# GIN's later layers in a message-passing kernel: y in two float16 parts, and two source tiles side by side in TensorE's column halves

## The reference, cut to what matters

```python
for l in range(4):
    S = segment_sum(X[src], dst)                       # over 3125 nodes
    Z = (1 + eps[l]) * X + S
    h = relu(bn(Z @ W1[l].T + b1[l], g1[l], bt1[l]))   # 128 -> 32 channels
    h = relu(bn(h @ W2[l].T + b2[l], g2[l], bt2[l]))   # 32 -> 32
    X = h @ W3[l].T + b3[l]                            # 32 -> 128
```

## Time and profile before

| what | us |
|---|---|
| median of 3 runs | 2328.12 (2324.81 to 2331.11) |
| the profiled execution, its own time | 2327.49 |
| its span, first to last instruction | 2325.7 |
| mean granted TensorE clock | 0.791 |
| busy: TensorE matmul / weight load | 1891.2 / 1354.5 |
| busy: DVE / ACT / POOL | 1375.0 / 1154.5 / 1360.8 |
| GIN, from its first products to its last read-out | 259.6 to 566.0 |

### The profile page before, as it was taken

One profiled execution on the slowest core, in us unless ns is written; L12 is line 12 of the kernel. 1 busy time (PEld: TensorE's weight loads), 2 busy tenths in 40 slices (PEclk: granted clock), 3 DMA queues, 4 the chain that ended last, 5 costly groups with the idle time before them and its releaser, 6 DMA issues. The chain is left out here.

```text
span 2325.7 us, 42471 instructions
## 1 busy us (share of the span) xinstructions
PE 1891.2 (81%) x8329; PEld 1354.5 (58%) x8329; DVE 1375.0 (59%) x4159; ACT 1154.5 (50%) x2623; POOL 1360.8 (59%) x1337
## 2 busy tenths in 40 slices
PE   3888667787798989998879989989986666667666
PEld 2666435554788878888655545545565455555554
DVE  6999681113543444344256666576567777777775
ACT  2999111112266666666436055064044666566663
POOL 1000137774477777777417758858826777777771
PEclk9999698788755555555579999999987777777777
DMA  0000101111344444444311111111132222222221
GB/s 11 0 0 0 44 4 17 18 18 12 105 120 119 117 119 118 117 119 119 103 33 18 17 16 18 17 16 18 20 133 72 65 64 64 64 65 65 64 64 38
DMA packets 195681, 128.56 MB, mean 55 GB/s; under 512 B 138365, under 2 KB 177854, under 8 KB 194587
## 3 DMA queue, kind: packets, MB, share of 16 engines
q0 software_dynamic: 40256, 60.21, 12.0%
q1 hardware_dynamic: 151388, 58.11, 9.9%
q10 hardware_dynamic: 3841, 8.16, 1.0%
HBM read 106.83 MB, written 13.34 MB: 52 GB/s over the span
## 5 line engine op out<-in xcount | busy, mean ns | idle before, releaser
L2157 POOL DMA_INDIRECT adj<-h_rows,adj x416 | 396.5, 953 | 153.4 <-issue 75.3
L1208 POOL DMA_INDIRECT work<-p_rows,small x416 | 395.3, 950 | 126.8 <-issue 99.7
L1584 POOL DMA_INDIRECT edge_rows<-pay,small x289 | 352.3, 1219 | 89.3 <-issue 85.4
L2374 PE MATMUL ps<-adj 128*128 128x125 f32 x928 | 209.1, 363 | 163.5 <-DVE adj L2252 161.2
L1392 PE MATMUL ps<-work 128*128 x1024 | 299.5, 446 | 43.5 <-ACT work L1328 39.6
L2374 PEld LDWEIGHTS ps<-adj 128*128 128x128 f32 x928 | 173.2, 256 | 255.5 <-issue 152.4
L1392 PEld LDWEIGHTS ps<-work 128*128 128x128 f32 x1024 | 232.9, 316 | 66.5 <-issue 60.7
L1285 DVE TENSOR_TENSOR work<-ps,work 128x256 f32<-128x256 f32 x256 | 108.6, 424 | 252.3 <-PE ps L1392 123.1
L1403 PE MATMUL ps<-small,work 128*128 128x64 f32 x1024 | 244.9, 393 | 11.2 <-DVE small L1274 7.7
L1403 PEld LDWEIGHTS ps<-small,work 128*128 128x128 f32 x1024 | 240.8, 323 | 20.4 <-DVE small L1274 15.3
L1946 PE MATMUL ps<-adj,work 125*128 (+2 forms) x1008 | 204.8, 359 | 20.5 <-DVE work L1675 20.5
(11 more groups left out here) (395 smaller groups left out, 3163.7 us busy)
## 6 DMA issues: line engine op xcount, KB each, us to landing
work<-dst_all SPq DMA_DIRECT2D x256, 64.0 KB
work<-edge_attr SPq DMA_DIRECT2D x256, 64.0 KB
edge_rows<-pay,small POOLq DMA_INDIRECT x425, 2.7
work<-p_rows,small POOLq DMA_INDIRECT x416
adj<-h_rows,adj POOLq DMA_INDIRECT x416
adj<-adj SPq DMA_DIRECT2D x232, 24.0 KB
pay<-edge_pay SPq DMA_DIRECT2D x106, 46.9 KB
adj<-edge_rows ACTq DMA_DIRECT2D x1, 2496.0 KB
```

The lines of the kernel that those rows point to most:

```text
L1208: eng.indirect_dma_start(gathered[:, at:at + D], None, p_rows[:, :], bass.IndirectOffsetOnAxis(ap=src_i[:, c:c + 1], axis=0)).then_inc(s_g ...
L1584: eng.indirect_dma_start(edge_rows[:, :], bass.IndirectOffsetOnAxis(ap=place[:, k:k + 1], axis=0), pay[:, k * ROW:(k + 1) * ROW], None).th ...
L2157: eng.indirect_dma_start(gathered[:, at:at + D], None, h_rows[:, :], bass.IndirectOffsetOnAxis(ap=row3_i[:, c, DST_C:DST_C + 1], axis=0)). ...
L2374: ins = eng.matmul(SUM[v % 2], msg[b][:, k * D:(k + 1) * D], hot[b][:, k * P:(k + 1) * P], start=k == 0, stop=k == PAIR - 1)
```

## The change

- In layers 1 to 3 y is kept in two parts of float16, 2 x 32 columns (`parts16`): ACT reads out the high part, DVE subtracts once. The columns of `joined` are multiplied by a power of two (`power`), which DVE makes from a bound on |y| (`size`), and `merge` for these layers holds the inverse (`size` / `TOP`). The bound is made by six matmuls into `BOUND` from `limits` (of gamma and beta), `sizes` (of `JOIN`) and `abs_b` (of `ROWS`).
- The adjacency product of layers 1 to 3 is written out: for each two slots, and each piece, one matmul with 64 columns of weights writes PSUM partitions 0 to 63 and the next, of the other slot, partitions 64 to 127. Slot 24 stands alone. The copies to `S` and the products with `merge` take 128 rows.
- b3 W1 no longer goes in by the degree: after a layer's last statistics TensorE writes the scaled bias row into the banks of y (two matmuls with one row of weights, 512 and 288 columns), and y is added to it.
- The degree row is saved in GIN, by SP, after layer 0's copies and ahead of the places. Layer 1's copies wait for it; the layernorm's transfer and wait go.
- `GIN_TURNS` is 14, so `EACH` is 13.

```diff
-GIN_TURNS = 17
+GIN_TURNS = 14
...
+    limits, tmp3, abs_b = s_(GH, GL - 1), s_(GH, GL - 1), s_(1, (GL - 1) * GH)
+    size, power = s_(D, (GL - 1) * GH), s_(D, (GL - 1) * GH)
+    bias_row = s_(1, (GL - 1) * GH)
...
+    parts16 = Words(T[3])(P, NT * 2 * GH, F16).rearrange("p (s c) -> p s c", c=2 * GH)
...
+    h, fold, sizes = y_(D, LONG), y_(D, D), y_(GH, (GL - 1) * GH)
...
-    merge = [t_(3 * GH + 1, WIDE) for _ in range(GL)]
+    merge = [t_(D, WIDE) for _ in range(GL)]
+    one_row = Words(G["extra"], 1536)(1, D)
...
-    JOIN, ROWS, OWN = (ps[:, 7, 0:(GL - 1) * GH], ps[0:3 * GH + 1, 7, 128:128 + (GL - 1) * GH],
+    JOIN, ROWS, OWN = (ps[:, 7, 0:(GL - 1) * GH], ps[0:1, 7, 128:128 + (GL - 1) * GH],
                        ps[:, 7, 256:256 + GL - 1])
+    BOUND = ps[:, 7, 384:384 + (GL - 1) * GH]
...
+            eng.wait_ge(s_sa, len(ACT_P))
+            eng.wait_ge(s_sv, len(DVE_P))
+            eng.dma_start(G["deg_row"][:, :], S[3 * GH:3 * GH + 1, :]).then_inc(s_deg, 16)
             eng.wait_ge(s_places, 1)
             eng.dma_start(places[:, :], place_i).then_inc(s_saved, 16)
             eng.wait_ge(s_saved, 16)
+            eng.wait_ge(s_deg, 16)
             for b in SETS:
                 fill(0, b)
             with eng.Fori(1, GIN_TURNS) as q:
...
-            for r in b3_row:
-                ins = eng.memset(r, 0.0)
-            step(ins)
+            step(eng.memset(one_row, 1.0))
...
-            for m in merge:
+            for m in merge[0:1]:
                 for i in range(3):
                     eng.tensor_copy(m[i * GH:(i + 1) * GH, 3 * GH:4 * GH], ident[i * GH:(i + 1) * GH, i * GH:(i + 1) * GH])
...
-            for l, r in enumerate(b3_row):
-                eng.tensor_copy(r[:, 3 * GH:3 * GH + 1], b3[:, l:l + 1]).then_inc(s_rows, 1)
             step(eng.tensor_scalar(eps, eps, 1.0, None, ALU.add))
+            gamma, beta = (vec[0:GH, i * GL:i * GL + GL - 1] for i in (4, 5))
+            step(eng.scalar_tensor_tensor(tmp3, beta, -1.0, beta, ALU.mult, ALU.max))
+            step(eng.scalar_tensor_tensor(limits, gamma, -1.0, gamma, ALU.mult, ALU.max))
+            step(eng.scalar_tensor_tensor(limits, limits, HIGHEST, tmp3, ALU.mult, ALU.add))
+            eng.wait_ge(s_join, 1)
+            eng.tensor_copy(sizes, JOIN[0:GH, :])
+            step(eng.tensor_copy(abs_b, ROWS))
+            eng.scalar_tensor_tensor(sizes, sizes, -1.0, sizes, ALU.mult, ALU.max)
+            eng.scalar_tensor_tensor(abs_b, abs_b, -1.0, abs_b, ALU.mult, ALU.max).then_inc(s_limits, 1)
             step(eng.tensor_scalar(w1e[:, 3 * GH:4 * GH], w1, eps[:, 0:1], None, ALU.mult))
 
             def affine(l, n):
@@ -712,10 +728,11 @@
                 at = slice((l - 1) * GH, l * GH)
                 for g in GROUPS:
                     rows = slice(g * GH, (g + 1) * GH)
-                    eng.tensor_copy(joined[l - 1][rows, rows], JOIN[rows, at])
+                    eng.tensor_tensor(joined[l - 1][rows, rows], JOIN[rows, at], power[rows, at], ALU.mult)
+                    eng.scalar_tensor_tensor(merge[l][rows, 3 * GH:4 * GH], ident[rows, rows], 1.0 / TOP,
+                                             size[rows, at], ALU.mult, ALU.mult)
                     eng.tensor_scalar(joined_e[l - 1][rows, rows], JOIN[rows, at], eps[rows, l:l + 1], None, ALU.mult)
-                cols = merge[l][:, 3 * GH:4 * GH]
-                eng.tensor_tensor(cols, cols, ROWS[:, at], ALU.add)
+                eng.tensor_tensor(bias_row[:, at], ROWS[:, at], power[0:1, at], ALU.mult)
                 step(eng.tensor_scalar(own[:, l - 1:l], OWN[:, l - 1:l], eps[:, l:l + 1], None, ALU.mult))
                 step(eng.tensor_tensor(vector(0, l), vector(0, l), own[:, l - 1:l], ALU.add))
...
                     y = ps[0:P, b, 0:(s1 - s0) * GH].rearrange("p (s c) -> p s c", c=GH)
                     eng.wait_ge(s_hi, l * 2 + b + 1)
+                    if l:
+                        eng.tensor_tensor(parts16[:, s0:s1, GH:2 * GH], y, parts16[:, s0:s1, 0:GH],
+                                          ALU.subtract).then_inc(s_parts, 1)
+                        continue
                     step(eng.tensor_tensor(rest[:, s0:s1, :], y, parts[:, s0:s1, 0:GH], ALU.subtract))
                     step(eng.tensor_copy(parts[:, s0:s1, GH:2 * GH], rest[:, s0:s1, :]))
                     eng.tensor_tensor(parts[:, s0:s1, 2 * GH:3 * GH], rest[:, s0:s1, :],
                                       parts[:, s0:s1, GH:2 * GH], ALU.subtract).then_inc(s_parts, 1)
                 if l == 0:
-                    eng.wait_ge(s_join, 1)
+                    eng.wait_ge(s_bound, 1)
+                    step(eng.tensor_scalar(size, BOUND, TINY, HUGE, ALU.max, ALU.min))
+                    step(eng.tensor_scalar(power, size, TWO23, None, ALU.mult))
+                    step(eng.tensor_tensor(size, size, power, ALU.add))
+                    step(eng.tensor_tensor(size, size, power, ALU.subtract))
+                    step(eng.reciprocal(power, size))
+                    step(eng.tensor_scalar(power, power, TOP, None, ALU.mult))
                     for k in range(1, GL):
                         weights(k)
                     eng.memset(h[GH:2 * GH, SHORT:LONG], 0.0).then_inc(s_tail, 1)
...
-                    eng.tensor_copy(S[0:YW - 1, c0:c0 + cw], ps[0:YW - 1, j, 0:cw]).then_inc(s_sv, 1)
+                    if l == 1:
+                        eng.wait_ge(s_deg, 16)
+                    tall = D if l else YW - 1
+                    eng.tensor_copy(S[0:tall, c0:c0 + cw], ps[0:tall, j, 0:cw]).then_inc(s_sv, 1)
...
+                    eng.activation((parts16 if l else parts)[:, s0:s1, 0:GH],
                                    ps[0:P, b, 0:(s1 - s0) * GH].rearrange("p (s c) -> p s c", c=GH),
                                    ACT.Copy).then_inc(s_hi, 1)
...
                 eng.matmul(JOIN[:, at], w3t[:, four], w_next, start=True, stop=True)
-                eng.wait_ge(s_rows, l)
-                eng.matmul(ROWS[:, at], b3_row[l - 1], w_next, start=True, stop=True)
+                eng.matmul(ROWS[:, at], b3[:, l - 1:l], w_next, start=True, stop=True)
                 ins = eng.matmul(OWN[:, l - 1:l], w1r[:, four], b3[:, l - 1:l], start=True, stop=True)
             ins.then_inc(s_join, 1)
+            eng.wait_ge(s_limits, 1)
+            for l in range(1, GL):
+                at = slice((l - 1) * GH, l * GH)
+                eng.matmul(BOUND[:, at], limits[:, l - 1:l].to_broadcast([GH, D]), sizes[:, at], start=True, stop=False)
+                ins = eng.matmul(BOUND[:, at], one_row, abs_b[:, at], start=False, stop=True)
+            ins.then_inc(s_bound, 1)
...
                         ins = eng.matmul(ps[0:P, b, at:at + tall], h[0:tall, i * P:c1], joined[l - 1][0:tall, 0:tall],
-                                         start=True, stop=True)
+                                         start=False, stop=True, skip_group_check=True)
...
                         four(i, i == 0)
+                    for j, c0, cw in PIECES:
+                        eng.matmul(ps[0:YW - 1, j, 0:cw], parts[:, 4 * FULL, 0:YW - 1], adj[:, FULL, c0:c0 + cw],
+                                   start=False, stop=True, skip_group_check=True).then_inc(s_sum, 1)
                 else:
-                    four(0, True)
-                    with eng.Fori(1, FULL) as i:
-                        four(i, False)
-                for j, c0, cw in PIECES:
-                    eng.matmul(ps[0:YW - 1, j, 0:cw], parts[:, 4 * FULL, 0:YW - 1], adj[:, FULL, c0:c0 + cw],
-                               start=False, stop=True, skip_group_check=True).then_inc(s_sum, 1)
+                    for n in range(0, NT, 2):
+                        for j, c0, cw in PIECES:
+                            for side in range(min(2, NT - n)):
+                                slot, at = n + side, side * 2 * GH
+                                ins = eng.matmul(ps[at:at + 2 * GH, j, 0:cw], parts16[:, slot, :],
+                                                 adj[:, tile_of(slot), c0:c0 + cw], start=n == 0, stop=slot >= NT - 2,
+                                                 skip_group_check=True)
+                            if n == NT - 1:
+                                ins.then_inc(s_sum, 1)
...
+                        tall = D if l else YW - 1
+                        ins = eng.matmul(ps[:, b, 0:d1 - d0], at_group(merge[l][0:tall, :], g), S[0:tall, n0:n1],
                                          start=False, stop=g == 3, skip_group_check=True)
...
                 spread(l, 1)
+                if l + 1 < GL:
+                    eng.wait_ge(s_zb[1], l * 2 + 2)
+                    if l == 0:
+                        eng.wait_ge(s_wl, 1)
+                    for b, s0, s1 in halves:
+                        row = bias_row[:, l * GH:(l + 1) * GH].unsqueeze(1).to_broadcast([1, s1 - s0, GH])
```

(8 more changed lines are left out.)

23 lines of the change are left out of this document (12 added, 11 removed).

## The result

| | before | changed |
|---|---|---|
| median of 4 runs (lowest to highest), us | 2326.5 (2323.1 to 2331.1) | 2289.9 (2288.1 to 2297.1) |
| ratio, 95% interval | | 0.984 (0.983 to 0.986) |
| profiled execution, us (span) | 2327.5 (2325.7) | 2297.1 (2295.4) |
| GIN ends (DVE's first addition of the layernorm) | 567.2 | 527.1 |

The account below looks back on a forecast made before the run. GIN was taken as bound by its compute chain, ending at 566.0 us with POOL 8.7 to spare. GIN -36.6, layernorm -0.9 and GENConv +0.4 made -37.1, from 2327.5 to 2290.4 us; 8-in-10 range 2284 to 2307.

Parts of the forecast that it names:

- Pairs: Adjacency product, layers 1 to 3: two matmuls in two column halves run at once, 0.19 us a pair, minus 15.9 a layer.
- the slow start stays: Start of each later layer's adjacency product: the first matmuls still run at 1.2 GHz, some 1.9 us extra.
- The parts of y and the bias matmuls: Turns between GIN layers: fewer parts of y save 1.7 us a turn, 5.1 in all; bias matmuls add 2.4 for three.
- Layer 0: GIN's first layer: added work for bound and weights delays the first scatter by 8.0 us, with 4 and 10 as ends.
- the half clock's 1.1 us: Layer 0, seven adjacency matmuls between two bins: after TensorE idles they take 2.6 us instead of 1.3 once, plus 1.1.
- Who ends GIN: End of GIN: POOL becomes last by 5.9 us, GIN ends at 529.4, minus 36.6; compute chain done at 523.5.
- Layernorm: Phase behind GIN: DVE no longer waits 1.98 us for the degree row, minus 0.9 us.
- GENConv: 24 scatters come back, 11.9 us of POOL, mostly into idle time: plus 0.4 us, ends 0 and 2.5.
- Rival B: Adjacency product: the halves take turns, 0.38 us a pair, total 2332.4 us; chance 0.08.
- C: Adjacency product: halves take turns and each paired load stands open, 0.29 us a matmul, total 2382.8 us; chance 0.04.
- Rival A: Adjacency product: a load stands open, 0.29 us a pair, plus 19.3 us, total 2309.7; chance 0.14.
- Rival D: Layer 0 costs 4 us instead of 8 and GENConv nothing: total 2286; inside the forecast's own case of 0.72.

Follow-up runs that it names:

- a_turns17: The changed kernel with GIN_TURNS = 17 instead of 14, on the second chip: ratio to the kernel before 0.998 (0.997 to 1.000).
- b_turns14: The kernel before with GIN_TURNS = 14 instead of 17 alone, on the second chip: ratio to the kernel before 1.000 (0.998 to 1.001).
- a_turns13: The changed kernel with GIN_TURNS = 13, the returned turn split over two GENConv layers, second chip: ratio to the kernel before 0.981 (0.978 to 0.984).
- a_one_half: The changed kernel with every slot's product in the same 64-column half, third chip: ratio to the kernel before 0.993 (0.989 to 0.996).
- a_again: The changed kernel run again without edit, on the second chip: ratio to the kernel before 0.986 (0.983 to 0.989).

## Why the prediction was right, and where its steps were off

**Pairs.** Right. The halves run at once and a warm pair takes 0.19 us. The products went from 35.2, 36.5 and 35.2 us to 19.1, 17.5 and 18.9: minus 16.1, 19.0 and 16.3 for 15.9 each. The step "the slow start stays" was too careful for layer 2, whose product starts at the full clock. The Trainium skill, TensorE: Matmul & The Clock Gate, Part 3: Packing small matmuls, gives 2.38 times for three strips. Here two halves gave 35.3 / 19.1 = 1.85 times, the start at half clock included in both, and 2 times once warm (0.19 us for a pair as for one). By the figure of the Trainium skill a pair would take 1.26 of one matmul's time, and the 84 pairs would make a layer's product some 4 us longer, an estimate. The same part of the Trainium skill has the rule that a load overlaps a running matmul only where the row groups differ. It isn't borne out by these rows: the row groups are the same, PE has no gap, and the loads lie beside it. They agree with the part's other words in the Trainium skill, by which a load may also be pulled ahead into a background weight buffer.

**The parts of y and the bias matmuls.** Minus 1.7 and plus 0.8 a turn were forecast, minus 2.7 in three. From the ReLU to the product's start the turns got shorter by 0.59, 0.95 and 0.67 us, 2.2 in all. The one turn shown before the change (7.22 us) was taken for all three; the other two took 6.92.

**Layer 0** was mis-sized: 8.0 us forecast, 4.0 measured, the lower end. Up to the parts' end it is 1.8 us (277.60 for 275.78; 1.7 forecast), the chain on the bound 2.15 (2.2 forecast). The term most in error is the twelve operations of 32 x 32 at 0.25 us, 3.0: DVE's weights took 7.2 us (279.67 to 286.86) for 6.9 before (275.69 to 282.55), so they cost 0.3. The timeline has them at 279.67, 279.78 and 279.88: the added one sits between two others 0.11 and 0.10 us apart, though each is recorded with some 0.2. I had priced them by their duration. They cost less even than their distance, which would be 1.2: the two operations that it now stands between started 0.19 to 0.21 us apart in nine of twelve places before, and 0.21 to 0.23 with it in between. The other term is the half clock's 1.1 us. It was seen on TensorE (7 matmuls in 2.05 and 2.30 us), but the places came no later than the fifth bin's scan did (4.0 us both), so the ranking on DVE covered it.

**Who ends GIN.** Right in kind: POOL, with the last landing near 525.2. First scatter 356.6 (360.5 forecast), GIN 40.0 us shorter (36.6), the difference being layer 0's. The slack was 11.0 us and not 5.9: the compute chain ended at 514.2 instead of 523.5, 4.0 of it from layer 0, 3.6 from the products and 2.2 from the stages behind the products, above all layer 0's and the last, which no term had (the first merge product took 1.05 us for 1.83, TensorE's last products of GIN 7.48 for 8.55), less 0.5 in the turns. a_turns17 and b_turns14 show the two chains one at a time.

**Layernorm.** Minus 0.9 was forecast, plus 0.3 measured. The wait for the degree row did go, but the step left out that a phase that waits for POOL finds TensorE cold: granted clock 0.50 from 528 to 534 where it was 1.00, and 8.54 us for 5.50 in its first product, where a_turns13, with no such wait, has 5.50 again.

**GENConv.** Plus 0.4 with 2.5 as the upper end; 2.2 measured. Idle times of 7.2 and 6.6 were forecast as 8 and 7. Behind the last reduction 105 scatters took 164.4 us (1512.19 to 1676.56) where 149.5 + 11.9 = 161.4 were forecast: two waits and one scatter of 1.99 us stand in the rows. The margin of 0.5 us was gone and POOL ends the phase.

**The sum** came out at 2290.4 for 2289.9 because GIN's 3.4 us too many, which are layer 0's, stand against 1.2 too few in the layernorm and 1.8 in GENConv. That they cancel to 0.4 us is luck; the mechanism, two halves at once and POOL as the last in GIN, is what the runs bear out. Rival B, and with it C, is shut out by the products' 17.5 to 19.1 us, beside 35.3 in a_one_half. Rival A's mechanism, a load that stands open, isn't seen. What spoke for it came true elsewhere: on the third and fourth chip TensorE doesn't keep up four instructions in 0.19 us for a whole layer. On the fourth GIN ends 12.5 us later than on the first, and the whole change still gives 0.986 (0.982 to 0.991) of the time before, though not all of that can be laid to GIN: 39.8 us in the medians, where GIN ends 27.6 before the 567.2 of the first two chips. Rival D's numbers for layer 0 were the right ones; its GENConv was not.

## What to carry to other kernels

Where two chains of nearly equal length share a phase, shortening one shows nothing until work is taken off the other: here each half of the change alone gave 1.000 and 0.998, and both together 0.984. Look for the slack that is left afterwards (11 us on the compute chain) and move work by less than a whole turn, into idle times that are smaller than one. Price a small independent operation by what it adds to the distance of its neighbours' starts, not by its duration: here twelve of 0.17 us added 0.3.

## What was not expected of the hardware

Two column halves of the array run at once, at 0.19 us for a pair as for one, and they do so even with seven matmuls in a row for each (25.5 us for 24.5). On two of four chips TensorE didn't keep up one matmul every 0.10 us: after some 15 us its loads came in bursts of four to six every 0.75 us. These chips also took 22 to 23% longer for the kernel before (2844 and 2857 us for 2326). And waiting for a slower engine at the end of a phase costs more than the wait: after 14.3 us of idling, seven products of TensorE took 8.54 us instead of 5.50, with a granted clock of 0.50 (level 1.2 GHz) for the first 6. How much it costs doesn't follow the length of the wait: 7.48 us after 12.6 (a_again), 6.93 after 48.6 (a_turns17).
